# A four-layer fp32 kernel: first stage and V, K and query projections as one sequence of units, weights laid out by the host

## The chip, the cores and the metric

The kernel runs on one core of one Trainium2 chip. The metric is the device time of one execution in microseconds; the figures shown are medians of several runs. TensorE multiplies (PE; its weight loads are PEld), VectorE (DVE), ScalarE (ACT) and GpSimd (POOL) work element by element, SyncE (SP) issues most transfers.

## What is computed

The input x holds 8 examples of 128 tokens and 512 features, in fp32. Four layers are added to it one after another:

```python
x = x + einsum('bsi,boi->bso', x, w0[adapter])                 # an own 512x512 weight for each example
x = x + attention(x)       # 32 query heads, 8 K/V heads of 128; q, k, v and the output are lora_linear; rope, causal mask
x = x + (x @ B_sel^T) @ A_sel^T                                # rank 16, by adapter
x = x + x @ W^T + b + 2 * (x @ A) @ Bm                         # a shared weight and a rank-16 adapter
# lora_linear: x @ w + (x @ a[id]) @ b[id], rank 16, an adapter for each example
```

## The kernel before

Each fp32 operand is split into a rounded high part and the remainder, "hi" and "lo" (both fp32r), and a product is made of three matmuls: hi·hi, hi·lo, lo·hi. ScalarE writes a hi part (a copy with rounding), then VectorE or GpSimd the lo part (a subtraction). TensorE contracts over partitions, so both operands need the feature on the partitions.

The program is written by hand in four blocks (L205, L559, L777, L1193). In a block each engine runs its own list of instructions in order; semaphores are the only links between them, and every engine waits at a block's end.

1. **First stage** (L205 to L495), over the 8 examples. `transposes(b)` (L260) turns x and the four 128-column tiles of this example's w0 (stored output-major) on TensorE into a ring of three PSUM banks; ScalarE and VectorE split each tile from there (`split`). `product(b)` (L277) is 12 matmuls into `ps_y`, VectorE adds them to `res` (`add`). One step later `turn_x1` transposes the sum, which is split into `x1t_hi` and `x1t_lo`; `adapters` multiplies it by the 48 columns of the q, k and v adapters, `pack_ax` and `turn_ax` bring these to `axt`. SP loads a w0 (1 MB) into one of two buffers when the transposes of two examples before are through, then the next x and three pieces of the adapter a, of 16 columns each. POOL issues tables and the gathers of bk, bv, bq and ao (DRAM to DRAM, by adapter). VectorE makes the sine, cosine and mask tables between the examples, and V block 0's weights are loaded and split in the last steps.
2. **V, K and first query projections** (L559 to L710). A unit is 12 matmuls of 512 columns and one or two for the adapter. Two V blocks of 8 units (one for each example), two K blocks of 8 (four heads, two token halves), and 4 query units. During each unit ScalarE and VectorE split one eighth of the next block (4 parts of `raw_w`, 4 of `raw_b`). V results are split into `v_hi`, `v_lo` (two buffers each) and stored to DRAM by SP; K results are multiplied by cosine and sine on VectorE, added on GpSimd into `kr` (two buffers) and stored to `k_rot`. Four PSUM banks take the units in turn. POOL first issues 16 gathers (bo, l3b).
3. **Attention** (L777 to L1115), 8 head groups of 8 examples. `load_wo` (L522) brings `wo` and the adapter `ao` (8 pieces of 64-byte runs) for each group.
4. **Last two layers** (L1193 to the end). W (L816, in `raw_w`) and `l2b_sel` are turned on TensorE with `turn` and split from PSUM; VectorE splits `bo_pack` (L1364), GpSimd `l3a_lo` (L1416).

The first stage's buffers, those of the projections and those of attention are allocated one stage after another, each in its own scope.

## Time and profile before

| what | value |
|---|---|
| median of 3 runs (lowest, highest) | 832.07 us (831.82, 832.17) |
| the profiled execution | 833.88 us, its span from first to last instruction 832.2 us |
| TensorE busy | 770.8 us, 93% of the span |
| VectorE, ScalarE, GpSimd busy | 541.0, 324.2, 282.4 us |
| DMA | 86.86 MB in 112748 packets, 60534 of them under 512 B |
| mean granted TensorE clock | 0.971 of full speed |
| first stage ends, first score, attention ends | about 100.2, 230.64, 767.3 us |

A row of the trace in order of time gives start and length in us, engine, line, operation, result<-operands by the program's names (the names are those of the buffer's first user: `raw_w` in the tail is w3), shapes and count; in brackets the idle time before it and what ended that. Matmuls overlap, so the distance between starts is what counts, not the length. A busy share is a mean over stages with different limits; what the change can move is read from the stage that it touches.

### The profile page before, as it was taken

Reading aid. Unit: us, or ns where it says so; the run is one execution under the profiler, and the core shown is the slowest. Engines: PE = TensorE matmul, PEld = TensorE weight load, DVE = VectorE, ACT = ScalarE, POOL = GpSimd, SP = SyncE. Lnnn points to the kernel's source line nnn. Section 1 sums busy time; section 2 is a strip of 40 time slices with the busy share of each in tenths; the row PEclk is TensorE's granted clock in tenths of the full one; section 3 lists DMA queues with packets and bytes.
Section 4 is the critical chain, followed back from the end, with each engine's and each line's share of the span. In section 5 each row is a group of like instructions: output and inputs, shape, how many; then the busy total and the mean of one; then the engine's idle time right before and its main releaser. Section 6 shows DMA issues by size and latency. Waiting matters only on the chain. (4 is left out here: it accounts for less than half of the span.)

```text
span 832.2 us, 13659 instructions
## 1 busy us (share of the span) xinstructions
PE 770.8 (93%) x4280; PEld 643.3 (77%) x4280; DVE 541.0 (65%) x1428; ACT 324.2 (39%) x924; POOL 282.4 (34%) x261
## 2 busy tenths in 40 slices
PE   4588898989689999999999999999999999997898
PEld 3477786778568888888888888888888888875586
DVE  2669643577766667667666767676767666754883
ACT  3255432311053435345335335334434443532540
POOL 5300030034445236336226326424523622410320
PEclk9889798999989999999999999999999999999999
DMA  9993178876405123314303502502412210810502
GB/s 258 315 268 96 52 209 220 234 223 194 146 2 139 39 65 85 95 30 96 113 0 116 124 0 63 153 23 63 126 51 59 67 38 3 164 13 4 128 19 84
DMA packets 112748, 86.86 MB, mean 104 GB/s; under 512 B 60534, under 2 KB 79126, under 8 KB 112454
## 3 DMA queue, kind: packets, MB, share of 16 engines
q1 hardware_dynamic: 110770, 79.83, 35.8%
q0 software_dynamic: 1792, 6.49, 2.4%
q8 instruction: 19, 0.31, 0.1%
q14 instruction: 19, 0.16, 0.1%
q10 hardware_dynamic: 148, 0.07, 0.0%
HBM read 71.40 MB, written 20.73 MB: 111 GB/s over the span
## 5 line engine op out<-in xcount | busy, mean ns | idle before, releaser
L921 POOL TENSOR_TENSOR prob<-prob,rinv 128x512 f32<-128x512 f32 x64 | 66.6, 1041 | 214.5 <-DVE rinv L1007 214.5
L870 ACT ACTIVATE prob<-sm,nmax 128x128 f32<-128x128 f32 x256 | 99.8, 391 | 77.8 <-DVE nmax L992 77.8
L1082 PE MATMUL ps_out<-wo_hi,ot_hi 128*128 128x512 f32 x256 | 106.5, 416 | 4.3 <-DVE ot_lo L969 2.4
L914 POOL TENSOR_TENSOR qt<-qc,qs 128x512 f32<-128x512 f32 x60 | 77.9, 1298 | 94.9 <-DVE qs L950 94.9
L859 ACT ACTIVATE ot_hi<-ps_o 128x512 fp32r<-128x512 f32 x64 | 38.1, 595 | 163.4 <-PE ps_o L1070 163.4
L1083 PE MATMUL ps_out<-wo_lo,ot_hi 128*128 128x512 f32 x256 | 100.7, 393 | 0.0
L80 PE MATMUL ps_q<-x1t_hi,blk_hi 128*128 128x512 f32 x240 | 100.7, 419 | 0.0
L1084 PE MATMUL ps_out<-wo_hi,ot_lo 128*128 128x512 f32 x256 | 100.6, 393 | 0.0
L81 PE MATMUL ps_q<-x1t_lo,blk_hi 128*128 128x512 f32 x240 | 95.6, 398 | 0.0
L82 PE MATMUL ps_q<-x1t_hi,blk_lo 128*128 128x512 f32 x240 | 95.4, 397 | 0.0
L950 DVE TENSOR_TENSOR qs<-ps_q,sin_t 64x512 f32<-64x512 f32 x120 | 82.6, 689 | 3.7
L992 DVE CUSTOM_DVE_ANT_0 sm<-ps_s,maskbias 128x128 f32<-128x128 f32 x256 | 59.0, 287 | 34.1 <-issue 33.6
L1050 PEld LDWEIGHTS ps_s<-kt,qt 128*128 128x128 f32 x512 | 67.7, 193 | 10.8 <-issue 5.4
L1050 PE MATMUL ps_s<-kt,qt 128*128 128x128 f32 x512 | 68.4, 277 | 5.2 <-PEq L559 5.2
L1082 PEld LDWEIGHTS ps_out<-wo_hi,ot_hi 128*128 128x128 f32 x256 | 48.1, 188 | 14.8 <-DVE ot_lo L969 4.0
L1084 PEld LDWEIGHTS ps_out<-wo_hi,ot_lo 128*128 128x128 f32 x256 | 48.0, 188 | 11.4
L989 DVE MEMSET gate<- 128x1 f32 x64 | 3.8, 59 | 79.8 <-PE ps_s L1050 79.8
L1083 PEld LDWEIGHTS ps_out<-wo_lo,ot_hi 128*128 128x128 f32 x256 | 48.3, 189 | 8.6
L853 ACT ACTIVATE pt_hi<-ps_t 128x512 fp32r<-128x512 f32 x64 | 38.1, 596 | 41.4 <-PE ps_t L1060 41.4
L82 PEld LDWEIGHTS ps_q<-x1t_hi,blk_lo 128*128 128x128 f32 x240 | 45.5, 190 | 11.0
L965 DVE TENSOR_TENSOR pt_lo<-ps_t,pt_hi 128x512 fp32r<-128x512 f32 x64 | 44.2, 691 | 13.5 <-ACT pt_hi L853 12.0
L81 PEld LDWEIGHTS ps_q<-x1t_lo,blk_hi 128*128 128x128 f32 x240 | 45.8, 191 | 8.3
(201 smaller groups left out, 1752.4 us busy)
## 6 DMA issues: line engine op xcount, KB each, us to landing
wo_raw<-in_L_cond_wo SPq DMA_DIRECT2D x8, 1024.0 KB, 5.4
raw_w<-in_L_cond_wq SPq DMA_DIRECT2D x8, 1024.0 KB, 6.5
w_raw<-in_L_cond_weight SPq DMA_DIRECT2D x7, 1024.0 KB, 6.7
raw_b<-bq_sel SPq DMA_DIRECT2D x56, 128.0 KB, 4.4
raw_b<-bkv_sel SPq DMA_DIRECT2D x16, 256.0 KB, 6.4
v_hi_d<-v_hi SPq DMA_DIRECT2D x16, 256.0 KB, 2.9
v_lo_d<-v_lo SPq DMA_DIRECT2D x16, 256.0 KB, 3.5
k_rot<-kr SPq DMA_DIRECT2D x16, 256.0 KB, 3.1
```

The lines of the kernel that those rows point to most:

```text
L80: pe.matmul(bank[:, :], w_hi[:, k, cols], x1t_hi[:, k, tok], start=(k == 0), stop=False)
L81: pe.matmul(bank[:, :], w_hi[:, k, cols], x1t_lo[:, k, tok], start=False, stop=False)
L82: pe.matmul(bank[:, :], w_lo[:, k, cols], x1t_hi[:, k, tok], start=False, stop=False)
L870: e = act.activation(prob[i][:, h, :], sm[:, h, :], ACT.Exp, bias=nmax[i][:, h:h + 1], scale=-1.0, accum_out=rsum[i][:, h:h + 1])
L914: pool.tensor_tensor(qt[:, half, h, :], qc[:, :], qs[:, :], ALU.add).then_inc(q_done, 1)
L921: pool.tensor_tensor(prob[i][:, :, :], prob[i][:, :, :], rinv[i][:, :].unsqueeze(2).broadcast_to([P, G, T]), ALU.mult).then_inc(prob_done, 1)
L950: dve.tensor_tensor(qs[to:to + 64, :], ps_q[i][at:at + 64, :], sin_t[to:to + 64, tok], ALU.mult).then_inc(q_mult, 1)
L992: m = dve.tensor_tensor_reduce(out=sm[:, h, :], in0=ps_s[i][:, h, :], in1=maskbias[:, b, :], scale=-1.0, scalar=3.0e38, op0=ALU.add, op1=A ...
L1050: mm = pe.matmul(ps_s[b % 2][:, h, :], qt[:, half, h, at:at + T], kt[:, b * T:(b + 1) * T], start=True, stop=True)
L1082: pe.matmul(ps_out[:, :], ot_hi[:, q], wo_hi[:, h, :], start=(h == 0), stop=False)
L1083: pe.matmul(ps_out[:, :], ot_hi[:, q], wo_lo[:, h, :], start=False, stop=False)
L1084: pe.matmul(ps_out[:, :], ot_lo[:, q], wo_hi[:, h, :], start=False, stop=(h == G - 1))
```

## The change

The host lays the weights out before the launch (`laid_out`): each w0 with the input feature first, in 128 rows of 8 KB; W and l2b with their feature first too; the q, k and v adapters a in one array with rows of 768 bytes; ao by head group, so that a group's piece has rows of 256 bytes. The kernel then has no transposes of w0, W and l2b; ScalarE takes hi parts straight from SBUF, VectorE the lo parts of three of the four chunks of w0 and GpSimd those of the fourth, in a ring of six chunks.

The first two blocks become one. In step s TensorE turns x(s+1), multiplies example s, turns x1(s-1), runs adapters (s-2), turns their rows (s-3), and from step 5 on runs V unit s-5; then units 8 to 35 follow with no block boundary. V block 0 is split in steps 1 to 4 (GpSimd takes its lo parts). The first 8 units use two PSUM banks, the later ones four. POOL issues only the gathers of bv ahead of its splits; the tables and the gathers of bk, bq, ao, bo and l3b follow when all w0 splits are done, ahead of K's rotations. SP waits for bk, bq and ao by semaphores of their own. Table steps of VectorE move from the first stage to units 3 to 15. Buffers of the front and of attention share one area of 80 KB at offsets given by hand (`at`), and `axo`, `l2a_sel`, `l2b_sel`, `l3a_sel` another. ao is loaded by one transfer for each group (`load_ao`), not eight.

The diff, cut:

```diff
-
-
-
...
+        field_at = (nc.sbuf_base + 31) // 32 * 32
+        sb(attn, "field", [P, 80 * 256 + 8])
+
+        def at(name, shape, kilobytes, dt=F32):
+            return nc.alloc_sbuf_tensor_at(name, shape, dt, offset=field_at + int(1024 * kilobytes))
+
...
+        def load_ao(dma, g):
+            dma.dma_start(ao_raw[:, :, :], ao_sel[bass.DynSlice(g, 1)].rearrange("a b p n -> p (a b) n")).then_inc(ao_in, 16)
+
...
+        LAG = 5
...
+            RING = 6
+            w0_raw = [at(f"w0_raw{i}", [P, KC, HID], 8 * i) for i in range(2)]
+            wt_hi = [at(f"wt_hi{i}", [P, HID], 16 + 4 * i, F32R) for i in range(RING)]
+            wt_lo = [at(f"wt_lo{i}", [P, HID], 18 + 4 * i, F32R) for i in range(RING)]
+            xt_hi = [at(f"xt_hi{i}", [P, KC * T], 40 + 4 * i, F32R) for i in range(2)]
+            xt_lo = [at(f"xt_lo{i}", [P, KC * T], 42 + 4 * i, F32R) for i in range(2)]
+            blk_hi.append(at("blk_hi1", [P, KC, GW], 48, F32R))
...
+                    def load_w0(b):
+                        a = sp.value_load(id_rows[0:1, 0, b:b + 1], min_val=0, max_val=w0.shape[0] - 1)
+                        src = w0[bass.DynSlice(a, 1)]
+                        if b >= 2:
+                            sp.wait_ge(w_lo_done, 3 * (b - 1))
+                            sp.wait_ge(w_lo_pool, b - 1)
+                        if b == 0:
+                            for k in range(KC):
+                                sp.dma_start(w0_raw[0][:, k, :], src[:, :, k * HID:(k + 1) * HID].rearrange("a p n -> p (a n)")).then_inc(w0_first_in[k], 16)
+                        else:
+                            sp.dma_start(w0_raw[b % 2][:, :, :].rearrange("p c n -> p (c n)"), src.rearrange("a p n -> p (a n)")).then_inc(w0_in[b % 2], 16)
+
+                    def load_x(b):
+                        sp.dma_start(res[:, b, :], x[b]).then_inc(x_in[b], 16)
+
+                    def load_a(b):
+                        pick = sp.value_load(id_rows[0:1, 1, b:b + 1], min_val=0, max_val=a_qkv.shape[0] - 1)
+                        sp.dma_start(a_raw[:, b, :, :, :].rearrange("p c n r -> p (c n r)"),
+                                     a_qkv[bass.DynSlice(pick, 1)].rearrange("a p n -> p (a n)")).then_inc(a_in[b], 16)
+
+                    sp.dma_start(id_rows[:, 0, :], lora_ids.rearrange("(a b) -> a b", a=1)).then_inc(lora_ids_in, 16)
+                    load_x(0)
+                    load_x(1)
+                    sp.wait_ge(lora_ids_in, 16)
+                    load_w0(0)
+                    sp.wait_ge(ids_in, 32)
+                    load_a(0)
+                    load_w0(1)
+                    load_a(1)
+                    load_x(2)
+                    load_block_w(sp, 0)
+                    for b in range(2, B):
+                        load_w0(b)
+                        if b + 1 < B:
+                            load_x(b + 1)
+                        load_a(b)
+                        if b == 3:
+                            sp.wait_ge(gathered_v, 16 * B)
+                            load_block_b(sp, 0)
+                        if b == 5:
+                            sp.wait_ge(blk0_lo_done, KC)
+                            load_block_w(sp, 1)
+                    sp.wait_ge(blk0_lo_done, UNITS)
...
+                    def w_split(b, k):
+                        if b == 0:
+                            act.wait_ge(w0_first_in[k], 16)
+                        elif k == 0:
+                            act.wait_ge(w0_in[b % 2], 16 * ((b + 1) // 2))
+                        j = KC * b + k
+                        if j >= RING:
+                            act.wait_ge(chunk_done, j - RING + 1)
+                        act.activation(wt_hi[j % RING][:, :], w0_raw[b % 2][:, k, :], ACT.Copy).then_inc(w_hi_done, 1)
+
...
+                    def copy_axt(b):
+                        act.wait_ge(axt_ready, b + 1)
+                        act.activation(axt[:, :, b * T:(b + 1) * T], ps_at[:, 0:3 * T].rearrange("p (n t) -> p n t", t=T),
+                                       ACT.Copy).then_inc(axt_done, 1)
+
...
+                    def unit(n):
+                        if n == 7:
+                            act.wait_ge(tab, 7)
+                            act.activation(sin_t[:, :], ang[:, :], ACT.Sin).then_inc(sines, 1)
+                        if n == 14:
+                            act.wait_ge(tab, 15)
+                            act.activation(cos_t[:, :], ang[:, :], ACT.Sin).then_inc(sines, 1)
+                        if n + UNITS < UNITS * (BLOCKS + 1):
+                            block_part(n + UNITS)
...
+                    for s in range(UNITS + LAG):
+                        if s + 1 < B:
+                            xt_split(s + 1)
+                            w_split(s + 1, 0)
+                            w_split(s + 1, 1)
+                        if 1 <= s <= B:
+                            a_split(s - 1)
+                        if s + 1 < B:
+                            w_split(s + 1, 2)
+                            w_split(s + 1, 3)
+                        if 1 <= s <= B:
+                            x1_split(s - 1)
+                        if 1 <= s <= 4:
+                            block_part(2 * s - 2)
+                            block_part(2 * s - 1)
+                        if 3 <= s <= B + 2:
+                            copy_axt(s - 3)
+                        if s >= LAG:
+                            unit(s - LAG)
+                    for n in range(UNITS, BLOCKS * UNITS):
+                        unit(n)
 
...
+                    def table_steps(n):
+
+                        for m in {3: (0, 1), 4: (2, 3), 5: (4, 5), 6: (6,), 7: (7, 8)}.get(n, (n + 1,) if 8 <= n <= 13 else ()):
+                            if m < 7:
+                                angle_step(0.0, m)
+                            else:
+                                angle_step(0.25, m - 7)
+                        if n == 14:
...
-                        if n == 2:
-
-                            dve.tensor_scalar(cos_t[:, :], cos_t[:, :], rope_cols[:, 1:2], None, ALU.mult).then_inc(scaled, 1)
-                            dve.tensor_scalar(sin_t[:, :], sin_t[:, :], rope_cols[:, 2:3], None, ALU.mult).then_inc(scaled, 1)
                         if n == VU:
                             dve.wait_ge(scaled, 2)
                         if n < VU:
                             dve.wait_ge(v_hi_done, n + 1)
...
+                    def gather_rows(ids_row, dst, src, done):
+                        for b in range(B):
+                            a = pool.value_load(id_rows[0:1, ids_row, b:b + 1], min_val=0, max_val=src.shape[0] - 1)
+                            pool.dma_start(dst[b:b + 1], src[bass.DynSlice(a, 1)]).then_inc(done, 16)
+
+                    def w_split(b):
+                        j = KC * b + KC - 1
+                        if b in (5, 6):
+                            pool.wait_ge(blk0_lo_done, 2 * (b - 2))
+                        pool.wait_ge(w_hi_done, j + 1)
+                        pool.tensor_tensor(wt_lo[j % RING][:, :], w0_raw[b % 2][:, KC - 1, :], wt_hi[j % RING][:, :].bitcast(F32),
+                                           ALU.subtract).then_inc(w_lo_pool, 1)
+
+                    def block_part(u):
+                        pool.wait_ge(raw_hi_done, u + 1)
+                        if u < KC:
+                            pool.tensor_tensor(blk_lo[0][:, u, :], raw_w[:, u, :], blk_hi[0][:, u, :].bitcast(F32),
+                                               ALU.subtract).then_inc(blk0_lo_done, 1)
+                        else:
+                            p = u - KC
+                            pool.wait_ge(w_lo_pool, u // 2 + 3)
+                            pool.tensor_tensor(blk_b[0][low, p, :], raw_b[low, p, :], blk_b[0][low, p, :].bitcast(F32),
+                                               ALU.subtract).then_inc(blk0_lo_done, 1)
+
+                    pool.wait_ge(ids_in, 32)
+                    gather_rows(1, bkv_sel[:, :, 1, :], bv, gathered_v)
+                    w_split(0)
+                    for s in range(7):
+                        if s + 1 < B:
+                            w_split(s + 1)
+                        if 1 <= s <= 4:
+                            block_part(2 * s - 2)
+                            block_part(2 * s - 1)
+
+                    pool.wait_ge(w_lo_done, (KC - 1) * B)
+                    pool.wait_ge(w_lo_pool, B)
+                    pool.dma_start(pos_i[:, :], pos.rearrange("b t -> (b t)").partition_broadcast(P)).then_inc(tables_in, 16)
+                    pool.dma_start(mask_u8[:, :], mask.rearrange("b t -> (b t)").partition_broadcast(P)).then_inc(tables_in, 16)
+                    pool.dma_start(causal[:, :], causal_c).then_inc(tables_in, 16)
+                    gather_rows(1, bkv_sel[:, :, 0, :], bk, gathered_k)
+                    gather_rows(1, bq_sel, bq, gathered_q)
+                    gather_rows(1, ao_sel.rearrange("g b p n -> b g p n"), ao, gathered_o)
+                    gather_rows(1, bo_sel, bo, last_gathered)
+                    gather_rows(2, l3b_sel, l3b, last_gathered)
                     for m in range(VU + G):
...
+                    def product(b):
+                        i = b % 2
+                        pe.wait_ge(xt_lo_done, b + 1)
+                        if b >= 2:
+                            pe.wait_ge(x1_done, b - 1)
+                        for k in range(KC):
+                            if k < KC - 1:
+                                pe.wait_ge(w_lo_done, (KC - 1) * b + k + 1)
+                            else:
+                                pe.wait_ge(w_lo_pool, b + 1)
+                            row = slice(k * T, (k + 1) * T)
+                            r = (KC * b + k) % RING
+                            pe.matmul(ps_y[i][:, :], xt_hi[i][:, row], wt_hi[r][:, :], start=(k == 0), stop=False)
+                            pe.matmul(ps_y[i][:, :], xt_hi[i][:, row], wt_lo[r][:, :], start=False, stop=False)
+                            pe.matmul(ps_y[i][:, :], xt_lo[i][:, row], wt_hi[r][:, :], start=False, stop=(k == KC - 1)).then_inc(chunk_done, 1)
+
+                    def turn_x1(b):
+                        pe.wait_ge(x1_done, b + 1)
...
+                        if n == 0:
+                            pe.wait_ge(blk0_lo_done, UNITS)
+                        elif u == 0:
                             pe.wait_ge(raw_lo_done, UNITS * blk)
-                        if 4 <= n < VU + 4:
-                            pe.wait_ge(v_lo_done, n - 3)
-                        elif n >= 4:
+                        if n < UNITS:
+                            pe.wait_ge(axt_done, n + 1)
+
+                        if 2 <= n < UNITS:
+                            pe.wait_ge(v_lo_done, n - 1)
+                        elif UNITS <= n < VU + 4:
+                            pe.wait_ge(v_lo_done, max(n - 3, min(n - 1, UNITS)))
+                        elif n >= VU + 4:
...
+                    for s in range(UNITS + LAG):
+                        if s + 1 < B:
+                            turn_x(s + 1)
+                        if s < B:
+                            product(s)
+                        if 1 <= s <= B:
+                            turn_x1(s - 1)
+                        if 2 <= s <= B + 1:
+                            adapters(s - 2)
+                        if 3 <= s <= B + 2:
+                            turn_ax(s - 3)
+                        if s >= LAG:
+                            unit(s - LAG)
+                    for n in range(UNITS, N_UNITS):
+                        unit(n)
 
         with ExitStack() as c:
...
                     for b in range(B):
                         a = sp.value_load(id_rows[0:1, 0, b:b + 1], min_val=0, max_val=l2a.shape[0] - 1)
-                        sp.dma_start(l2b_sel[b * R:(b + 1) * R, :], l2b[bass.DynSlice(a, 1)].rearrange("a r n -> (a r) n")).then_inc(l2_in, 16)
-                        sp.dma_start(l2a_sel[:, :, b, :], l2a[bass.DynSlice(a, 1)].rearrange("a (c p) r -> p (a c) r", p=P)).then_inc(l2_in, 16)
+                        sp.dma_start(l2b_sel[:, :, b, :], l2b[bass.DynSlice(a, 1)].rearrange("a p c r -> p (a c) r")).then_inc(l2_in, 16)
+                        sp.dma_start(l2a_sel[:, :, b, :], l2a[bass.DynSlice(a, 1)].rearrange("a p c r -> p (a c) r")).then_inc(l2_in, 16)
                     for b in range(B):
                         a = sp.value_load(id_rows[0:1, 2, b:b + 1], min_val=0, max_val=l3a.shape[0] - 1)
...
                     pe.wait_ge(l3a_in, 16 * B)
                     for k in range(KC):
@@ -1256,7 +1326,7 @@
                     o = ps_h[1][:, :]
                     pe.wait_ge(l2a_lo_done, 1)
                     for k in range(KC):
-                        pe.wait_ge(turn_lo_done, k + 1)
...
-        "L3_cond_lora_As", "L3_cond_lora_Bs"]
+def laid_out(inputs):
+
+
+    def by_rows(a):
+        n, rows, cols = a.shape
+        return np.ascontiguousarray(a.reshape(n, rows // P, P, cols).transpose(0, 2, 1, 3))
+
+    w0 = by_rows(np.swapaxes(inputs["L0_cond_weight"], 1, 2))
+    w3 = by_rows(np.swapaxes(inputs["L3_cond_W"], 0, 1)[None])[0]
+    a_qkv = np.stack([by_rows(inputs[f"L1_cond_a{n}"]) for n in "qkv"], 3)
+    ao = inputs["L1_cond_ao"]
+    n, rows, rank = ao.shape
+    heads = inputs["L1_cond_wq"].shape[1] // inputs["L1_cond_wk"].shape[1]
+    ao = ao.reshape(n, rows // (heads * P), heads, P, rank).transpose(0, 1, 3, 2, 4)
...
```

## Rows read from the trace of the kernel before

**Rows 1.** Table of stages: length, busy time by engine, clock, DMA share, GB/s.
```profile
0.00:100.50 100.50, 70.39 (x408) 60.65 (x408) 61.50 (x119) 40.79 (x89) 18.21 (x40) 0.88 0.70 204
...
230.60:260.00 29.40, 26.94 (x135) 22.36 (x136) 20.23 (x63) 16.48 (x49) 16.82 (x13) 0.91 0.19 45
260.00:764.00 504.00, 498.97 (x2927) 421.08 (x2927) 337.11 (x1057) 215.60 (x688) 199.95 (x163) 1.00 0.27 69
```

**Rows 2.** Waits, 0 to 250 us: who waited for whom, total, times, longest.
```profile
PE ps_ring L274 <- DMA w_raw<-in_L_cond_weight: 18.6, 4, 10.1
```

**Rows 3.** TensorE in order of time, one step: start, length, instructions, idle before.
```profile
60.87 0.62 PE L274 MATMUL ps_ring<-ident,res 128*128 128x128 f32 x4
61.33 1.04 PE L274 MATMUL ps_ring<-ident,w_raw 128*128 128x128 f32 x8
...
63.98 0.47 PE L285 MATMUL ps_y<-wt_hi,xt_hi 128*128 128x512 f32 x1
...
67.15 0.27 PE L306 MATMUL ps_a<-a_hi,x1t_hi 128*128 128x48 f32 x1
...
68.86 0.62 PE L274 MATMUL ps_ring<-ident,res 128*128 128x128 f32 x4
```

**Rows 4.** TensorE in order of time at the unit and block boundaries.
```profile
109.12 0.40 PE L705 MATMUL ps_p<-blk_b,axt_v 128*128 128x512 f32 x1
...
127.32 0.39 PE L705 MATMUL ps_p<-blk_b,axt_v 128*128 128x512 f32 x1
131.49 0.79 PE L700 MATMUL ps_p<-blk_hi,x1t_hi 128*128 128x512 f32 x1 [3.78 <-DVE blk_b L646]
...
136.77 0.44 PE L705 MATMUL ps_p<-blk_b,axt_v 128*128 128x512 f32 x1
...
213.04 0.50 PE L80 MATMUL ps_p<-x1t_hi,blk_hi 128*128 128x512 f32 x1 [2.95 <-DVE blk_b L646]
...
230.64 2.05 PE L1050 MATMUL ps_s<-kt,qt 128*128 128x128 f32 x8 [5.20 <-PEq L559]
```

**Rows 5.** TensorE in order of time: first weight tile, first product.
```profile
9.57 2.98 PE L274 MATMUL ps_ring<-ident,w_raw 128*128 128x128 f32 x12 [4.46 <-DMA w_raw<-in_L_cond_weight]
...
21.54 0.78 PE L285 MATMUL ps_y<-wt_hi,xt_hi 128*128 128x512 f32 x1
```

**Rows 6.** The same table for three stretches of the first stage.
```profile
10.00:70.00 60.00, 42.79 (x245) 36.63 (x244) 38.16 (x66) 23.61 (x46) 12.72 (x26) 0.86 0.99 294
...
20.00:30.00 10.00, 9.40 (x47) 7.78 (x46) 8.37 (x13) 4.57 (x8) 5.91 (x12) 0.79 1.07 388
...
50.00:60.00 10.00, 8.11 (x61) 7.14 (x58) 7.70 (x16) 6.39 (x11) 0.00 (x0) 1.00 1.02 244
```

**Rows 7.** ScalarE, VectorE and GpSimd in order of time: splits of SBUF operands.
```profile
100.73 2.19 ACT L608 ACTIVATE blk_b<-raw_b 128x512 fp32r<-128x512 f32 x4 [0.29 <-PEq L205]
...
101.40 2.51 DVE L634 TENSOR_TENSOR blk_b<-raw_b,blk_b 64x512 fp32r<-64x512 f32 x4 [3.21 <-ACT blk_b L608]
...
776.07 3.60 DVE L1364 TENSOR_TENSOR bo_pack<-raw_b,bo_pack 64x512 fp32r<-64x512 f32 x4
...
777.24 1.27 POOL L1416 TENSOR_TENSOR l3a_lo<-l3a_sel,l3a_hi 128x512 fp32r<-128x512 f32 x1 [21.46 <-ACT l3a_hi L1322]
```

**Rows 8.** POOL's issues in order of time; a wait; the landing of v_lo stores.
```profile
101.87 0.49 POOL L674 DMA_DIRECT2D bo_sel<-in_L_cond_bo  x1 [70.63 <-issue]
103.03 0.49 POOL L676 DMA_DIRECT2D l3b_sel<-in_L_cond_lora_Bs  x1 [0.67 <-issue]
...
109.95 0.49 POOL L676 DMA_DIRECT2D l3b_sel<-in_L_cond_lora_Bs  x1 [0.84 <-issue]
111.87 1.02 POOL L674 DMA_DIRECT2D bo_sel<-in_L_cond_bo  x1 [1.43 <-issue]
...
ACT v_hi L627 <- DMA v_lo_d<-v_lo: 20.1, 8, 5.4
...
DMA to landing us min/median/max: 2.9/3.7/7.4
```

765 lines of the change are left out of this document (330 added, 435 removed).

## The prediction

> **What bounds the kernel now.** I first read the table of stages, to see where TensorE is not busy. The attention stage (260 to 764 us) holds 499 us of TensorE work in 504 at full clock, and the change leaves its matmuls alone: nothing is to be won there. The first 100.5 us hold 70.4 us of it at a mean clock of 0.88 [rows 1]. So the front, up to the first score at 230.6 us, decides. Then the waits of TensorE: 18.6 us for adapter weights, one of them 10.1 [rows 2]. Then one example of the first stage in order of time. From 60.87 to 68.86 us is one step, 7.99 us: turning x takes 0.46, turning the four weight tiles and waiting for the ring's banks 2.65 (61.33 to 63.98), product and x1 3.17, adapters and their rows 1.71 [rows 3]. Last, the boundaries. V block 0 ends at 127.7 us, the next starts at 131.49 after 3.8 of idling, the query units at 213.04 after 2.95, and the first score is at 230.64 after 5.2 [rows 4].
>
> **The weights' layout and the first stage.** Without the 128 weight transposes and the ring an example costs TensorE 7.99 - 2.65 = 5.34 us, eight of them 42.7. A V unit lasts 3.03 (109.12 to 127.32 are six) [rows 4], and eight of them, one example's unit five steps behind its product, are now in the same sequence: 24.3. The first product starts at 21.54 today; its first weight piece landed at 9.57 [rows 5]. They now come in rows of 2 KB and are split straight from SBUF, so I put the first product at 10. Cold matmuls come 0.43 us apart and warm ones 0.23; twelve cold ones cost 2.5 us, the gap by which the unit ending at 137.2 exceeds 3.03 [rows 4]. TensorE alone would therefore end V block 0 at 10 + 2.5 + 42.7 - 0.5 + 24.3 = 79 us. That is the lower bound.
>
> **The transfers of the first stage.** Before the last example's product the queues must move w0 8 MB, x 2, a 0.8, the gathered V rows 0.5, two weight blocks 2, one row block 1 and about 0.7 of V stores: 15 MB. From 10 to 70 us the DMA engines were full at 294 GB/s, at best 388 and at worst 244 in ten microseconds [rows 6]. So 15 MB take 51 us, with 2 ahead and 1.5 for the splits: product 7 starts at 54.5. Behind it TensorE still has that product 2.8, x1, adapters and rows of the last examples 6.2 (of the 3.17 and 1.71 above, 0.35 is an x1 turn, 1.34 and 0.37 the parts of the second) and units 2 to 7, 18.2: 27.2 us. V block 0 ends at 82 us by this and at 79 by TensorE, and I take 82. The ends: 76 with a product at 8 and no cold start, 92 at 244 GB/s. That compares with 127.7, so 45.7 us are gone. The a rows, 24 transfers of 64-byte runs, become eight with 768-byte runs. I count nothing more for it, since the rate above includes them.
>
> **The splits.** ScalarE in a step of the first four: x, four weight chunks, x1, two block parts, one wide adapter copy and the small a, some nine at the 0.52 us at which its copies follow one another: 4.8 us, under 5.34. VectorE: x, three chunks, sum and x1 at 0.6 each, a and packing about 1.0: 4.6. GpSimd takes the fourth chunk and two parts of V block 0, 1.3 us each: 3.9 [rows 7]. Each is hidden by TensorE's 5.34. If GpSimd is alone with its port, this costs nothing.
> Against that stand rows where GpSimd and VectorE both read two SBUF operands: four bo_pack splits took 3.60 us beside one GpSimd split of 1.27, where four of the same shape took 2.51 alone [rows 7]. So a GpSimd split can cost VectorE 1.1. With three per step VectorE needs 4.6 + 3.3 = 7.9, 2.6 over TensorE, in four steps 10 us. I take zero beyond the transfers' pace, because in these steps the transfers leave 5 to 8 us per example; the rest is a rival.
> The Trainium skill, "SBUF — State Buffer", section "Who interferes with whom", says that a VectorE instruction with two SBUF inputs and a GpSimd one that reads SBUF exclude each other for their whole length. The trace agrees in size; the rule speaks against this change, for it turns PSUM sources into SBUF ones and puts GpSimd beside them.
>
> **What moves later.** POOL's queue: tables, bk, bq and ao gathers went out by 31 us under cover of the first stage; now they are issued behind the last weight split, near 52. With bo and l3b they are 3 + 40 issues; at 1.12 us from one to the next [rows 8] they last until 99. Units need the tables from unit 3 (about 66 us), SP needs bk at unit 7 (about 82; ready at 69). K's rotations stand behind the gathers and are due near 116. Covered; their bytes (5.7 MB) are not. From the end of block 0 to the first score today's kernel takes 230.6 - 127.7 = 102.9 us, of which 28 units are 84.9, the boundary 5.2 and stalls 12.8. The stalls come from stores: ScalarE waited 20.1 us for v_lo stores (3.7 us typical, 7.4 at most), and the block parts queued behind it on ScalarE were late [rows 4, 8]. I keep 102.9 and add 7 for the denser transfers. Bounds: -9 if the two gaps go (3.8 + 2.5 + 2.95), and +16.5 if each pair of stores takes 7.4 us, since two buffers then pace a unit at (7.4 + 1.2)/2 = 4.3, 1.27 over, in 13 units. Block 0 now rotates through two banks, so it feels a late store sooner. First score: 82 + 103 + 7 = 192, for 230.6: 38.6 us less. The new waits on SP (gathered_k, gathered_q, gathered_o) hold V and K stores and next blocks; by the times above each is met first, cost nothing, and without that cover as long as the gather is late.
>
> **Attention and tail.** ao comes in one transfer per group instead of eight; TensorE is busy there in any case, and the first group's start (26.9 of 29.4 us busy [rows 1]) depends on other things: 0, bounds -1 and +1. Placing buffers by hand costs nothing. In the tail the w3 and l2b transposes go. VectorE's splits of them were nearly back to back and bo_pack's 3.60 us [rows 7] follow all the same: -0.5, bounds -3 and 0.
>
> **The sum.** Span 832.2 - 38.6 - 0.5 = 793.1 us, 39.1 less. The profiled execution took 833.9, the median is 832.07; with the same difference 793.0.
>
> **The rivals.**
> - Clean cover: the first stage runs at TensorE's pace and the store stalls vanish, 79 + 103 - 9 = 173, or 774 us. For it: 388 GB/s were seen [rows 6]. Against: the free stretches of today's queues are now filled.
> - Stores saturate: first score 192 - 7 + 16.5 plus up to 8 for a slow first stage, 202 to 210, 803 to 811 us. For it: store waits of up to 5.4 us [rows 8], with fewer transfers beside them than there will be.
> - The shared port: VectorE paces steps 1 to 4 at 7.9 us, 10 us of which some 2 are inside the transfers' margin: 801 us.
> - The sequence doesn't overlap: block 0's parts come late, and unit 0 holds products 5 to 7, because TensorE's queue is in order. One stall of 10 us: 803.
> - Slower than before: POOL's gathers spread out under full queues. At 1.12 us they leave 17 us before K's rotations are due, so from 1.55 on they delay K. To cost 39 us more they must reach 2.5; at 2.6 the kernel takes 835 us. One step of 1.92 is in the trace (109.95 to 111.87) [rows 8], the 16 gathers there are otherwise near 1.12 apart.
>
> **How the numbers follow.** Forecast 0.52 (782 to 802), clean cover 0.20, saturated stores 0.15, port 0.08, no overlap 0.02, slower 0.03. The range 771 to 813 takes in the first five: from block 0 at 76 without the gaps (first score 170) to block 0 at 92 with 16.5 of store stalls (211.5). A measurement tells 0.2% apart, 1.7 us; faster by more 0.96, within 0.01, slower 0.03.
>
> **What would show it.** Right: no weight transposes, 5.3 us steps, product 7 at 50 to 60 us, V block 0's last unit at 76 to 92, first score at 180 to 205, an unchanged attention length (537 us). Wrong if steps last over 7 us with VectorE waiting beside GpSimd, if ScalarE waits much over 20 us for v_lo stores, if GpSimd is still gathering when K's first unit ends, or if attention changes by more than 2 us.

## The result and the profile after

The changed kernel takes 808.01 us (median of 4 runs, 805.03 to 810.83), the one before 832.12 in the same comparison: ratio 0.9708, 95% interval 0.9671 to 0.9745, so 24 us less. The profiled execution took 807.25 us and its span is 805.6, for 833.88 and 832.2 before. The forecast was 793.0 with a range of 771 to 813. The time lies inside the range, but outside the forecast's own 782 to 802, in the place of the rival "stores saturate" (803 to 811). TensorE is busy for 748.7 us instead of 770.8. The same 86.8 MB move in 75228 packets, 26791 of them under 512 B, instead of 112748 and 60534.

The table of stages, whose columns are those of [rows 1]; the third and fourth lines answer to its last two:

```profile
0.00:76.00 76.00, 62.28 (x333) 50.61 (x334) 52.04 (x96) 41.41 (x82) 35.59 (x45) 0.98 0.85 263
76.00:102.00 26.00, 12.33 (x54) 9.76 (x53) 11.23 (x18) 7.48 (x12) 11.38 (x22) 0.78 0.78 255
...
204.00:233.40 29.40, 26.93 (x134) 22.33 (x135) 19.96 (x63) 16.42 (x49) 16.82 (x13) 0.90 0.14 46
233.40:737.40 504.00, 498.84 (x2931) 421.61 (x2930) 337.51 (x1057) 215.57 (x688) 199.84 (x163) 1.00 0.25 69
```

Attention is what it was: 26.93 and 498.84 us of TensorE work for 26.94 and 498.97. The new thing is the second line, 26 us in which TensorE works for 12.3. The waits of TensorE up to 205 us say what it is; they answer to [rows 2]:

```profile
PE ps_v L762 <- DVE blk_b L576: 13.7, 1, 13.7
PE ps_s L1123 <- PEq L286: 8.1, 1, 8.1
PE ps_xt L687 <- DMA res<-in_x: 5.4, 2, 4.0
PE ps_v L80 <- DVE blk_b L576: 4.3, 2, 2.3
PE ps_y L703 <- DVE wt_lo L484: 3.7, 5, 1.9
PE ps_y L703 <- POOL wt_lo L636: 3.1, 3, 2.7
```

TensorE in order of time: the first product, the last matmuls of V units 0, 1, 2 and 7, then the starts of V block 1, the first K block, the queries and attention. They answer to [rows 4, 5]:

```profile
8.29 0.77 PE L703 MATMUL ps_y<-wt_hi,xt_hi 128*128 128x512 f32 x1 [0.61 <-DVE wt_lo L484]
...
51.96 0.40 PE L765 MATMUL ps_v<-blk_b,axt 128*128 128x512 f32 x1
...
60.29 0.40 PE L765 MATMUL ps_v<-blk_b,axt 128*128 128x512 f32 x1
60.52 0.40 PE L703 MATMUL ps_y<-wt_hi,xt_hi 128*128 128x512 f32 x1
...
68.19 0.40 PE L765 MATMUL ps_v<-blk_b,axt 128*128 128x512 f32 x1
...
87.46 0.40 PE L765 MATMUL ps_v<-blk_b,axt 128*128 128x512 f32 x1
101.53 0.80 PE L762 MATMUL ps_v<-blk_hi,x1t_hi 128*128 128x512 f32 x1 [13.67 <-DVE blk_b L576]
...
131.07 0.55 PE L80 MATMUL ps_v<-x1t_hi,blk_hi 128*128 128x512 f32 x1 [2.31 <-DVE blk_b L576]
...
183.50 0.50 PE L80 MATMUL ps_v<-x1t_hi,blk_hi 128*128 128x512 f32 x1 [1.98 <-DVE blk_b L576]
203.98 2.04 PE L1123 MATMUL ps_s<-kt,qt 128*128 128x128 f32 x8 [8.07 <-PEq L286]
```

V block 0 ends at 87.9 us instead of 127.7: 40 us won. The first score starts at 203.98 instead of 230.64: 26.7 us are left of them. The 13.2 between went to the idling of 13.67 between the V blocks (3.78 before), to the 8.07 at the block's end (5.20), and to K's first matmuls, which ran at the lower clock behind 2.31 us of idling (0.43 us apart for the 0.23 of the rest; the granted clock is 0.91 from 131 to 151 us). The waits ahead of K and of the queries are 1.2 us shorter. V block 1's first unit ran at the lower clock in both kernels.

The idling, followed back. ScalarE in order of time shows that the last part of V block 1, `blk_b`, was not late for its data; it stood in ScalarE's queue behind a `v_hi` copy that waited for its buffer, and behind a sine:

```profile
82.32 0.62 ACT L425 ACTIVATE blk_b<-raw_b 128x512 fp32r<-128x512 f32 x1
97.15 0.60 ACT L440 ACTIVATE v_hi<-ps_v 128x512 fp32r<-128x512 f32 x1 [14.21 <-DMA v_lo_d<-v_lo]
97.77 1.28 ACT L430 ACT_TABLE_LOAD   x1
99.11 1.06 ACT L430 ACTIVATE sin_t<-ang 128x1024 f32<-128x1024 f32 x1
100.07 0.61 ACT L425 ACTIVATE blk_b<-raw_b 128x512 fp32r<-128x512 f32 x1
```

The buffer was held by a store. SP's queue, in order of time, shows the pair of stores that took 5 us each only to be issued:

```profile
79.82 0.37 SPq L340 DMA_DIRECT2D v_hi_d<-v_hi  x1
80.23 0.76 SPq L340 DMA_DIRECT2D v_lo_d<-v_lo  x1
83.18 4.96 SPq L340 DMA_DIRECT2D v_hi_d<-v_hi  x1
88.18 4.73 SPq L340 DMA_DIRECT2D v_lo_d<-v_lo  x1
98.50 0.37 SPq L340 DMA_DIRECT2D v_hi_d<-v_hi  x1
```

The view of the tile `v_lo_d` gives the landing times of the `v_lo` stores, 16.8 us at most for 7.4 before [rows 8]:

```profile
DMA to landing us min/median/max: 2.8/4.0/16.8
```

In those microseconds GpSimd sends the bq and ao rows, 256 KB each (first and last of 16), beside a 1 MB load of K's weights issued at 76.33:

```profile
69.44 0.49 POOL L629 DMA_DIRECT2D bq_sel<-in_bq  x1 [0.67 <-issue]
...
87.91 0.50 POOL L629 DMA_DIRECT2D ao_sel<-in_ao  x1 [0.64 <-issue]
```

The table of stages for 80 to 85 us has the DMA engines full:

```profile
80.00:85.00 5.00, 5.00 (x23) 4.04 (x22) 4.81 (x6) 1.12 (x2) 2.50 (x5) 1.00 1.01 362
```

Before, these gathers went out by 31 us, in the first stage.

### The profile page after: what moved, and what is told of

Same layout as the page of the kernel before. It is cut to its first block and busy times, and to the rows that moved or that the text cites. A ratio compares the mean times of both kernels' runs of the same rounds, so it can differ in the third digit from the quotient of the medians.

```text
span 805.6 us, 13257 instructions
## 1 busy us (share of the span) xinstructions
PE 748.7 (93%) x4132; PEld 622.4 (77%) x4132; DVE 537.8 (67%) x1412; ACT 321.5 (40%) x908; POOL 307.5 (38%) x276
## 2 busy tenths in 40 slices
DMA packets 75228, 86.84 MB, mean 108 GB/s; under 512 B 26791, under 2 KB 44359, under 8 KB 73975
## 5 line engine op out<-in xcount | busy, mean ns | idle before, releaser
L1123 PEld LDWEIGHTS ps_s<-kt,qt 128*128 128x128 f32 x512 | 67.6, 193 | 13.7 <-issue 8.2
L1155 PEld LDWEIGHTS ps_out<-wo_hi,ot_hi 128*128 128x128 f32 x256 | 48.1, 188 | 14.1 <-DVE ot_lo L1042 4.0
L80 PEld LDWEIGHTS ps_q<-x1t_hi,blk_hi 128*128 128x128 f32 x240 | 45.9, 191 | 8.5
```

What stands on the lines that cost most here:

```text
L80: pe.matmul(bank[:, :], w_hi[:, k, cols], x1t_hi[:, k, tok], start=(k == 0), stop=False)
L1123: mm = pe.matmul(ps_s[b % 2][:, h, :], qt[:, half, h, at:at + T], kt[:, b * T:(b + 1) * T], start=True, stop=True)
L1155: pe.matmul(ps_out[:, :], ot_hi[:, q], wo_hi[:, h, :], start=(h == 0), stop=False)
```

## The experiments

All ratios are to the kernel before, measured beside it on the same chip. e1 to e4 were measured together, e5 to e8 together and e9 to e12 together, so between these groups the ratios are to be compared, not the times. e1 and e2 leave a part of the work out; all others do the whole. "Gap" is TensorE's idling between the V blocks, "store" the time from issue to landing of the slowest v_lo store, both of the one profiled execution.

| run | us | ratio, 95% interval | gap | store |
|---|---|---|---|---|
| the kernel before | 832.12 | 1 | 3.8 | 7.4 |
| the change | 808.01 | 0.9708 (0.9671, 0.9745) | 13.7 | 16.8 |
| e1_no_gathers | 792.19 | 0.9506 (0.9454, 0.9557) | 2.2 | 6.4 |
| e2_small_wk | 802.92 | 0.9663 (0.9616, 0.9711) | 8.1 | 13.2 |
| e3_four_buffers | 797.79 | 0.9589 (0.9541, 0.9636) | 2.2 | 17.7 |
| e4_units_behind | 809.11 | 0.9743 (0.9688, 0.9798) | 2.4 | 14.1 |
| e5_paced_gathers | 805.79 | 0.9691 (0.9652, 0.9730) | 2.2 | 7.5 |
| e6_four_paced | 797.32 | 0.9610 (0.9576, 0.9645) | 2.2 | 9.8 |
| e8_vector_splits | 805.86 | 0.9693 (0.9657, 0.9729) | 12.6 | 15.8 |
| e7_layout_only | 825.76 | 0.9925 (0.9887, 0.9963) | 2.9 | 7.9 |
| e9_two_layouts | 823.09 | 0.9862 (0.9825, 0.9900) | 6.0 | 8.8 |
| e11_late_gathers | 811.31 | 0.9726 (0.9690, 0.9762) | 2.6 | 7.3 |
| e10_three_adapter_loads | 811.62 | 0.9727 (0.9694, 0.9761) | 14.0 | 17.2 |
| e12_four_wide | 793.60 | 0.9512 (0.9479, 0.9545) | 2.2 | 18.0 |

**Who makes the stores late (e1, e2)?** e1 takes the bq and ao gathers away by reading the tables themselves, without the choice by adapter; e2 leaves the gathers and loads only a corner of K's first weight block, 1 MB less.

```diff
-    bq_sel = nc.dram_tensor("bq_sel", (B, R, KVH * GW), F32, kind="Internal").ap()
+    bq_sel = bq
...
-                    gather_rows(1, bq_sel, bq, gathered_q)
```

> The changed kernel without the gathers of bq and ao: bq_sel and ao_sel are the adapter tables themselves, in their own order, so examples get other adapters' rows for the queries and the output adapter (that part of the computation is changed). All the rest stands. Theory A: the 13.7 us stall of TensorE between the two V blocks comes from these 4 MB, which POOL's queue moves at 69 to 90 us beside the V stores. Then the stall falls to about 4 us (the 3.8 of the kernel before), the largest v_lo landing from 16.8 to under 8 us, and the kernel takes 807 - 10 = 797 us. Theory B: the 1 MB load of wk, issued at 76.3 us on the stores' own queue, does it. Then the stall stays over 9 us and the time within 3 us of 807.

```diff
+                if n == 2:
+                    dma.dma_start(raw_w[:, 0:1, 0:GW // 2], src[:, 0:1, 0:GW // 2]).then_inc(raw_w_in, 16)
```

> The changed kernel with the load of K block 0's weights (wk, 1 MB, issued just ahead of V unit 4's store) cut to its first 128 rows and 256 columns; the K block is then computed from stale weights (that part is changed). Theory B (that load in front of the stores): the stall between the V blocks falls to about 4 us, 797 us. Theory A (the gathers): the stall stays over 9 us, the time falls by 3 us at most (1 MB at 290 GB/s is 3.4 us). If both do it together, each of the two runs takes about half: 5 us.

Without the gathers the gap is 2.2 us, no v_lo store takes more than 6.4 to land, and the kernel is 15.8 us faster than the changed one. (SP's waits for these gathers go with them, but none of them shows in SP's queue of the changed kernel.) With the small weight load the gap is 8.1; the 5 us against the changed kernel are within the intervals. So both share the queues with the stores, and the gathers' share is the larger.

**Is it the latency or the bytes (e3, e5, e6)?** e3 gives `v_hi` and `v_lo` four buffers each. e5 keeps two and spreads the gathers: bq one per V unit from unit 4, ao behind V units 12 to 15 and K rotations 0 to 3, bo and l3b behind rotations 4 to 11. e6 has both.

```diff
-                            if n >= 2:
-                                act.wait_ge(v_out[n % 2], 32 * (n // 2))
+                            if n >= 4:
+                                act.wait_ge(v_out[n % 4], 32 * (n // 4))
```

> The changed kernel with four buffers each for v_hi and v_lo instead of two (the two new ones lie at 32 to 40 KB, free after the last product), so that ScalarE waits for the store of four units before. Nothing is left out. If the stall is the store's latency and nothing else (theory C), ScalarE may run four units ahead, 12 us, of a store of 16.8: the stall falls from 13.7 to under 4, and the kernel takes 797 us or less. If throughput of the queues is short over the whole V phase (theory D), the stall only moves to later units or into K: 804 to 808.

```diff
-                    gather_rows(1, bq_sel, bq, gathered_q)
+                    for b in range(B):
+                        pool.wait_ge(v_lo_done, 4 + b)
+                        gather_rows(1, bq_sel, bq, gathered_q, b)
```

> All of the changed kernel's work is done; only GpSimd's gathers are spread out. The bq rows are gathered one per V unit from unit 4 on, the ao rows four beside V units 12 to 15 and four after the first K rotations, the bo and l3b rows after K rotations 4 to 11, and the ao tile is loaded at K unit 9. Theory (the gathers crowd the V stores, what counts is how many stand in the queues at once): the longest landing of a v_lo store falls from 16.8 us to under 8, the wait between the V blocks from 13.7 us to 2 to 4, and the time to 792 to 799 us, near the run without the bq and ao gathers (792.2). Rival (the bytes themselves cost it, wherever they lie): the wait moves to the start of K or of the queries, the three waits for blk_b still add up to over 14 us, and the time stays at 803 to 810 us.

> All work is done: the paced gathers of the run above and, with them, four v_hi/v_lo buffers instead of two. Theory: with pacing the stores land in time and the second pair of buffers adds nothing more than 3 us; 789 to 797 us, waits for blk_b together under 9 us. Rival (each mends another half: pacing frees the loads of the K block, the buffers free the ring): both gains add, 783 to 789 us. If the spread gathers collide with the loads of K's block: above 798 us.

In e3 a store still lands after 17.7 us, yet the gap is 2.2 and the kernel 10 us faster than the changed one: what cost time was that a late store stops ScalarE's queue after two units. A part of the idling moved on, as theory D had it: TensorE's waits for blk_b ahead of K and the queries are 9.0 us, for 4.3 in the changed kernel. e5 did to the stores what its theory said (7.5 us at most, gap 2.2) and yet gained nothing that can be told from the changed kernel. Its start of K, TensorE in order of time:

```profile
124.06 0.80 PE L80 MATMUL ps_v<-x1t_hi,blk_hi 128*128 128x512 f32 x1 [8.60 <-DVE blk_b L577]
```

Its waits for blk_b ahead of K and the queries add up to 13.8 us, for 4.3 in the changed kernel; with the gap they are 16.0, for 18.0. ScalarE now waited for v_lo stores up to 103.6 and 114.8 us (5.19 and 5.41). That is the rival: the bytes were moved, and the wait moved with them. e6, with both edits, is level with e3, so the pacing adds nothing to the buffers either.

**Does it matter that V units run inside the first stage (e4)?** Here unit s-11 follows step s instead of s-5.

```diff
-        LAG = 5
+        LAG = 11
```

> The changed kernel with V unit 0 in step 11 instead of step 5, that is, all eight V units of block 0 behind the first stage's products; loads, splits and the single sequence of instructions are as they are. My step: TensorE's first-stage work (42.7 us) and V block 0 (24.3) share one stretch bounded by TensorE after 27 us, so nothing of the units fills idle time late in the stage; then this costs little, 0 to 5 us (807 to 812). If the overlap is what brings the gain (TensorE idles between products once the units are gone because transfers and splits pace a step at 6.5 us or more), three units' time is lost: 9 us or more, 816 and up.

e4 cannot be told from the changed kernel. TensorE waited 8.1 us inside V block 0 instead of 13.7 behind it. When a unit starts mattered little as long as the stores ended the chain.

**Does GpSimd slow VectorE (e8)?** All 32 subtractions of w0 on VectorE:

```diff
-                            if k < KC - 1:
-                                pe.wait_ge(w_lo_done, (KC - 1) * b + k + 1)
-                            else:
-                                pe.wait_ge(w_lo_pool, b + 1)
+                            pe.wait_ge(w_lo_done, KC * b + k + 1)
```

> The changed kernel with all 32 layer-0 weight subtractions on VectorE; GpSimd keeps block 0's. All work is done. Theory (VectorE and GpSimd slow each other where both subtract in SBUF): the mean of the wt_lo subtraction on VectorE falls from 925 ns to 690 to 800, the 8 more cost 5.5 to 6.5 us and the falls of the 24 give 3 to 5.5 back, TensorE's 3.1 us of waits for GpSimd's wt_lo go and some for VectorE's come; product 7 starts within 2 us of 60.5 and the time is 805 to 811 us. Rival (VectorE's slow subtractions have another cause, as the waits of its queue or PSUM): the mean stays over 880 ns, VectorE is 6 us or more longer in the stage, product 7 starts after 63 and the time is over 811 us.

VectorE's groups up to 62 us (busy, mean ns), the changed kernel's two first, then those of e8:

```profile
L484 DVE TENSOR_TENSOR wt_lo<-w_raw,wt_hi 128x512 fp32r<-128x512 f32 x24 | 21.6, 925 | 9.4 <-ACT wt_hi L395 9.2
L499 DVE TENSOR_TENSOR a_lo<-a_raw,a_hi 128x192 fp32r<-128x192 f32 x7 | 5.7, 821 | 0.0
```

```profile
L483 DVE TENSOR_TENSOR wt_lo<-w_raw,wt_hi 128x512 fp32r<-128x512 f32 x32 | 23.2, 763 | 8.4 <-ACT wt_hi L394 8.4
...
L498 DVE TENSOR_TENSOR a_lo<-a_raw,a_hi 128x192 fp32r<-128x192 f32 x7 | 2.4, 349 | 0.0
```

24 subtractions beside GpSimd's eight cost VectorE 21.6 us; all 32 cost 23.2, with GpSimd's eight splits of V block 0 beside them in both. The subtractions that read PSUM (xt_lo) kept their 685 ns. GpSimd's eight took about 1.5 us each and relieved VectorE of 1.6 us in all, or less than nothing with the a_lo row. This is no accident of one execution: the six other runs with the changed kernel's first stage (e1, e2, e3, e5, e6, e12) show means of 911 to 975 ns. In e10, below, GpSimd's eight are in place too, but VectorE waits longer for ScalarE, and the mean is 782 ns and that of a_lo 350: the loss depends on when the two engines meet. What it costs in time is not shown. Product 7 started at 57.58 us in e8 and at 60.52 in the changed kernel, but the six others start it at 57.74 to 59.86, and e8's time is that of the changed kernel within the intervals.

**What does each part of the change give, on top of the kernel before (e7, e9, e11, e10)?** e7: only w0 feature-major, TensorE turns nothing but x. e9: also the adapters in one load a row (its runs are of 768 bytes; the expectation's 1536 is an error). e11: also the bq and ao gathers held back until row 6 is split. The stages, their order and the last layers are those of before in all three.

```diff
-                            act.activation(xt_hi[i][:, :] if j == 0 else wt_hi[i][:, j - 1, :], ps_ring[m % 3][:, :],
+                            act.activation(xt_hi[i][:, :] if j == 0 else wt_hi[i][:, j - 1, :], ps_ring[b % 3][:, :] if j == 0 else w0_raw[b % 2][:, j - 1, :],
```

> The kernel before with one part of the change alone: the layer-0 weights come feature-major from the host, TensorE turns only x in the first stage, and the two splits read w0_raw instead of the PSUM ring. Adapter loads, the separate V, K and query stages, GpSimd's gathers and the last stage are those of before. Theory (the transposes are what the change gains, the merged sequence adds little): 8 steps lose 2.65 us each, 832 falls to 808 to 814 us, 18 to 24 us less, so that the layout alone is worth about as much as the whole change. Rival (transfers pace the first stage as soon as TensorE doesn't, with the three small adapter loads a step still there): TensorE waits more than 15 us for w0 or x in the stage and the time is 818 to 826 us. Rival (the merge carries half of it): 820 us with no such waits.

```diff
-                        for n, src in enumerate((aq, ak, av)):
-                            sp.dma_start(a_raw[:, b, :, n, :],
-                                         src[bass.DynSlice(pick, 1)].rearrange("a (c p) r -> p (a c) r", p=P)).then_inc(a_in[b], 16)
+                        sp.dma_start(a_raw[:, b, :, :, :].rearrange("p c n r -> p (c n r)"),
+                                     aq[bass.DynSlice(pick, 1)].rearrange("a p n -> p (a n)")).then_inc(a_in[b], 16)
```

> The kernel before with two layouts of the change: the layer-0 weights feature-major, as in the run with that alone (825.8 us, TensorE waited 25.4 us for x), and the three adapters of a row as one load of 1536-byte runs instead of three of 64-byte runs. Theory (the 64-byte runs of the adapter loads hold up w0 and x behind them in SP's queue and in the DMA engines): the waits for x fall from 25.4 us to under 10, ScalarE's for w0 from 31.4 to under 12, the first V product starts at 80 to 87 us instead of 95.9, and the time is 811 to 818 us. Rival (the bytes pace the stage, as 1.3 MB a step and 32 gathers at some 300 GB/s, whatever the packets): within 4 us of 825.8. Rival (VectorE's chain after each product sets the step, its tables too): waits for x go and the step stays over 7 us, 820 us.

```diff
+                    pool.wait_ge(tile_lo_done, TILES * (B - 1))
                     for b in range(B):
```

> The run with the two layouts (the weights and the adapters), and GpSimd issues the 16 gathers of bq and ao only once VectorE has split row 6 of the first stage. Theory (these 4 MB, read and written, stand in the way of w0 and x in the stage): waits for x under 5 us, the first V product 3 to 8 us earlier than with the two layouts alone, 805 to 812 us, the level of the changed kernel, whose merged order then is worth next to nothing. Rival (with the packets gone the DMA engines have room for them): within 2 us of the run with the two layouts. Rival (they end after the stage and hold up its end): slower than that run by 2 us or more.

The first V product, TensorE in order of time, in e7, e9 and e11 (100.76 in the kernel before):

```profile
95.92 0.76 PE L697 MATMUL ps_p<-blk_hi,x1t_hi 128*128 128x512 f32 x1 [0.97 <-PEq L205]
```

```profile
88.39 0.76 PE L696 MATMUL ps_p<-blk_hi,x1t_hi 128*128 128x512 f32 x1 [0.97 <-PEq L205]
```

```profile
78.58 0.76 PE L697 MATMUL ps_p<-blk_hi,x1t_hi 128*128 128x512 f32 x1 [0.97 <-PEq L205]
```

Without the transposes alone the stage is 4.8 us shorter, not 21, and the kernel 6; the first rival (818 to 826 us) had it so. The rest turned into a wait for transfers, as e7's waits, one stall of TensorE and the SP issues before it show:

```profile
PE ps_ring L266 <- DMA res<-in_x: 25.4, 6, 7.7
...
ACT wt_hi L341 <- DMA w_raw<-in_L_cond_weight: 31.4, 6, 11.8
```

```profile
41.12 1.12 PE L266 MATMUL ps_ring<-ident,res 128*128 128x128 f32 x4 [7.59 <-DMA res<-in_x]
```

```profile
27.77 0.43 SPq L225 DMA_DIRECT2D res<-in_x  x1
28.96 0.38 SPq L228 DMA_DIRECT2D a_raw<-in_L_cond_aq  x1
29.86 1.28 SPq L228 DMA_DIRECT2D a_raw<-in_L_cond_ak  x1
31.27 6.42 SPq L228 DMA_DIRECT2D a_raw<-in_L_cond_av  x1
38.47 0.35 SPq L223 DMA_DIRECT2D w_raw<-in_L_cond_weight  x1
38.86 0.43 SPq L225 DMA_DIRECT2D res<-in_x  x1
```

An adapter load of 64-byte runs held SP's queue for 6.42 us, and w0 and x stood behind it. Packed (e9), TensorE's waits for x fall to 18.4 us and ScalarE's for w0 to 21.3; the stage is 7.5 us shorter again, but the kernel, by the ratios, some 5 us, with intervals that overlap a little. That is less than this run's theory wanted. Holding the gathers back (e11) brings 9.8 us in the stage and 11.8 in the kernel, with intervals well apart: TensorE waits 11.2 us for x, all of it for the first two rows, and ScalarE 10.3 for w0. Now the stage is 22.2 us shorter than before, about the 8 x 2.65 = 21.2 of the transposes, and the kernel is level with the changed one.

e10 undoes one part of the changed kernel: the adapters in three loads again.

```diff
+                        for n, src in enumerate((aq, ak, av)):
+                            sp.dma_start(a_raw[:, b, :, n, :],
```

> The changed kernel with one part undone: the adapters come as three loads a row with 64-byte runs, as before the change. All else, order too, is the changed kernel's. Theory (the packed adapter load is a large part of the gain): TensorE's waits for x and w0 in the first stage grow from 5.4 us to 15 to 25, product 7 starts at 70 to 80 us instead of 60.5, and the time is 815 to 825 us. Rival (in the changed kernel nothing waits on the adapter rows, since the order of its loads puts x and w0 two rows ahead and the gathers come later): product 7 within 3 us of 60.5, 806 to 811 us.

Its ratio is 0.0019 over the changed kernel's, within the intervals. TensorE waits 9.4 us for x instead of 5.4, and product 7 starts at 62.76, 2.2 us later than in the changed kernel. So the packing, of use in the old order, is worth at most a little in the new one, where x and w0 are issued further ahead.

**A better version (e12).** Four buffers as in e3, and V kept in DRAM token by token, so that a store writes runs of 2048 bytes instead of 512.

```diff
-    v_hi_d = nc.dram_tensor("v_hi_d", (KVH, T, B, D), F32, kind="Internal").ap()
+    v_hi_d = nc.dram_tensor("v_hi_d", (T, B, KVH * D), F32, kind="Internal").ap()
...
-                                sp.dma_start(dst[g, :, b, :].rearrange("g t d -> t g d"),
+                                sp.dma_start(dst[:, b, h * GW:(h + 1) * GW],
```

> All work is done: the changed kernel with four v_hi/v_lo buffers (797.8 us in its run) and V kept in DRAM token by token, so that a store writes 2048-byte runs instead of 512-byte ones, while the loads of the attention stage read 512-byte runs instead of 2048-byte ones. Theory (the 65 thousand small packets of the V and K part crowd the loads of its blocks): the waits for blk_b fall from 11.2 us to under 7, 791 to 796 us, and the attention stage keeps its 536 to 537 us since its transfers are hidden. Rival (runs of 512 bytes are no worse than longer ones there): 796 to 800 us. If the attention's narrower loads come late: its length grows by 2 us or more and the time is over 800 us.

793.6 us, 0.9512 of the kernel before and some 2% under the changed one. (The expectation's 65 thousand small packets are too many: from the first V store to the first score e3 moves 27.7 thousand packets of all sizes and e12 17.0 thousand.) TensorE at the start of V block 1 and of attention, then ScalarE's wait for stores:

```profile
87.83 0.65 PE L764 MATMUL ps_v<-blk_hi,x1t_hi 128*128 128x512 f32 x1 [2.20 <-DVE blk_b L575]
...
191.09 2.05 PE L1125 MATMUL ps_s<-kt,qt 128*128 128x128 f32 x8 [8.07 <-PEq L286]
```

```profile
ACT v_hi L439 <- DMA v_lo_d<-v_lo: 1.8, 3, 0.9
```

The waits for `blk_b` are 7.7 us together for 11.2 in e3, not under the 7 of the theory. Attention keeps its length, so the narrower loads are hidden there. Against e3 the wide stores bring some 6 us, but the intervals meet (0.9545 and 0.9541) and the two runs were not measured together: likely, not shown.

## Why the prediction was right, and where it was off

The range held and the forecast number did not: of the 39.1 us that I forecast 24.1 came. Up to V block 0's end 39.8 us of the forecast 45.7 were won. What followed cost more than I had allowed, and that the time lies within 771 to 813 rests on the room that I had left there for store stalls. It lies in the place of "stores saturate", but by another course than that rival's, so this is in part luck.

- **First product at 10:** 8.29, 1.7 us earlier.
- **A step costs TensorE 5.34 us:** from the end of V unit 0 (51.96) to that of unit 1 (60.29) are 8.33 us, less a unit of 3.03, 5.30. Right.
- **Product 7 at 54.5:** 60.52, and 57.74 to 59.86 in the six runs with the same first stage. TensorE alone would have been there at about 54: 8.3, seven steps of 5.34, units 0 and 1 (6.1) and the 2.5 of cold matmuls, less 0.5. Behind its first product it idled for 7.6 us in small waits, 1.4 for x and 6.2 for wt_lo. The transfers gave 292 GB/s from 10 to 60 us, as I assumed, but at a share of 0.92, so they alone no longer set the pace. Two things that I had at nothing show in the rows of GpSimd, VectorE and TensorE:

```profile
14.98 0.50 PE L703 MATMUL ps_y<-wt_hi,xt_hi 128*128 128x512 f32 x1 [2.71 <-POOL wt_lo L636]
...
29.46 1.45 DVE L499 TENSOR_TENSOR a_lo<-a_raw,a_hi 128x192 fp32r<-128x192 f32 x1
30.65 3.08 POOL L642 TENSOR_TENSOR blk_lo<-raw_w,blk_hi 128x512 fp32r<-128x512 f32 x2
30.83 1.75 DVE L484 TENSOR_TENSOR wt_lo<-w_raw,wt_hi 128x512 fp32r<-128x512 f32 x1
32.63 0.50 PE L703 MATMUL ps_y<-wt_hi,xt_hi 128*128 128x512 f32 x1 [1.92 <-DVE wt_lo L484]
```

  GpSimd issues its eight bv gathers ahead of its first split and comes to it only at 13.65 us, though ScalarE had the hi part ready at 10.04: the 2.71 us of waiting in the first row. And beside GpSimd's splits VectorE's a_lo and wt_lo take 1.45 and 1.75 us, for 0.35 and 0.68 alone: 1.92 us of waiting here and 0.85 at 45.54, the shared port of my rival. e8 takes the first away and a part of the second (GpSimd's splits of V block 0 stay); TensorE then waits 3.2 us for x, and product 7 starts at 57.58, hardly below the six. So neither is shown to move product 7, and why product 7 is later in the changed kernel's own execution than in those six stays open.
- **27.2 us behind it to V block 0's end:** 60.52 to 87.9 are 27.3. The end at 82 became 87.9, in the bounds of 76 to 92. (The 76 does not follow from its own terms: 79, less 2 for the product at 8 and less 2.5 of cold start, is 74.5.)
- **102.9 + 7 us from there to the first score:** 116.1. This is the step that failed in size. The base was right: e11, which leaves the projections as they were, takes 103.1 from block 0's end (105.1) to its first score at 208.25. The 7 for denser transfers should have been 13.2. The mechanism is the one that I named, a late store that stops ScalarE before the next block's parts. The bound for it was made from a pair of stores at 7.4 in each of 13 units, and what came was one store of 16.8 us at a block's end. My sign for it, "ScalarE waits much over 20 us for v_lo stores", did not show: the total is 19.7 us, for 20.1 before [rows 8]. Four waits instead of eight, one of 14.2, cost what the same total had not. Nor is the longest wait a better sign: in e5 it is 5.4, of 15.2 in six, and TensorE's waits for blk_b are still 16.0.
- **POOL's gathers covered, their bytes not:** K's rotations were not late (the last gather was issued at 107.64, the first K unit ended near 136), so the rival on the slower side did not come about. The gathers cost 15.8 us (e1), more than twice my 7; four buffers (e3) win 10 back with the gathers in place.
- **What the gathers' move also gave:** I priced the transfers of the first stage at 15 MB, and had thereby left the moved gathers out of it, without saying how much hangs on that. In the old order half of it does: e7, with neither that move nor the packing, gives 6 us, e9 with the packing some 11, e11 with both some 22. No run has the changed kernel's order with the gathers in the first stage. "I count nothing more" for the adapter rows holds in the changed order (e10) and not in the old one (e9, some 5 us, at the edge of what was measured).
- **What the merged sequence gives:** I had expected nearly all that V block 0 wins to stay. Against e11, V block 0 ends 17.3 us earlier in the changed kernel (87.9 for 105.1), the span is 3.9 us shorter, and the ratios overlap. With stores that stop ScalarE less, more of the earlier end reaches the first score: from one to the other are 112.1 us in e3 and 105.4 in e12, for 116.1 in the changed kernel and 103.1 in e11. I did not try e11 with four buffers, which would bound that share from the other side.
- **Boundary 5.2:** 8.07, and 8.1 in all merged kernels but e1 (6.7). 2.9 us that I had not foreseen. It lies behind the last work that the trace shows: GpSimd's last rotation ends at 199.42 us and the next block starts at 203.9, 4.5 us later, for 1.7 before. I didn't find its cause.
- **Attention 0:** 536.2 us from first score to its end, for 536.7. Right.
- **Tail -0.5:** +0.6. The transposes are gone, but the mean clock was 0.92 from 740.2 us on, for 0.97 before, and the four matmuls at the tail's start took 2.81 us in this execution and 1.95 in those of e1, e3 and the kernel before. From these matmuls to the end are 64.2 us here, 63.6 before, 63.4 in e1 and 62.7 in e3.
- **The sum:** 82 + 110 = 192 for 203.98 is 12.0 short, attention 0.5 the other way, the tail 1.1: 793.1 to 805.6. Of the 12.0, 5.9 arose up to V block 0's end and 6.1 behind it.

That e12 takes 793.6, nearly the number that I had predicted for the change, confirms nothing: it has two edits more, and its V block 0 ends at 85.7, 3.7 us later than I said, with 105.4 from there to the first score, 4.6 less than my 110. The two nearly cancel.

## What to carry to other kernels

Work taken off the bounding engine is worth only what the transfers of that stage allow: here 21 us of transposes gave 6, and some 22 once the adapter loads were packed and 16 gathers had left the stage. Work moved under another stage's cover takes its bytes with it; ask whose buffers those bytes will hold up, how many units the ring lasts, and what stands in the same queue behind the copy that waits for a buffer. When latency is the trouble, more buffers (10 us here) beat pacing the traffic (nothing measurable).

## What the runs showed of the hardware

- Crowded transfers show at the issuing engine: SP was held 4.96 and 4.73 us by the issue of two stores of 256 KB in 512-byte runs (share of the DMA engines 1.01 from 80 to 85 us); the other 30 such issues of the changed kernel take 0.37 to 1.65. In e3 one took 10.3 us. In e12, with runs of 2048 bytes, none took over 0.95, though its longest landing is 18.0 us. In e7 one adapter load of 32 KB in 64-byte runs took 6.42.
- VectorE's subtraction with two SBUF operands took 676 ns at the least and up to 1758 beside GpSimd's; a small one of 192 columns 349 on the mean in e8 and 821 in the changed kernel. The same instruction from PSUM did not change (685 and 684). The Trainium skill, "SBUF — State Buffer", section "Who interferes with whom", says that such pairs exclude each other, and these rows agree in direction: moving a quarter of them to GpSimd relieved VectorE of 1.6 us of 23.2. In e10 the same split cost VectorE 18.1 us for its 24, so it matters when they meet.
- 303 GB/s moved in e7 from 10 to 60 us and 344 in e9, each at a full share (1.01 and 0.97): with the adapters packed the same engines carried more.
